# Layer 3's messages between the two steps of scaling: from SBUF into a PSUM bank

## The chip, the cores and the metric

The kernel runs on one core of a Trainium2 chip. The metric is the device time of one execution in microseconds (us), the median of several runs. TensorE (PE) does matmuls, VectorE (DVE), ScalarE (ACT) and GpSimd (POOL) do elementwise work; POOL also issues the gathers from tables in HBM (its indirect DMAs), and SyncE issues the plain DMAs.

## The reference, cut to what matters

Four graph layers follow one another over 6,250 nodes of 256 features and 100,000 edges that are sorted by their destination node. The change is in the last one, layer 3, an attention over edges with 4 heads of 64 features:

```python
h_fwd = h @ W_forward.T          # 6250 x 64
h_rev = h @ W_reverse.T
messages = h_fwd[src] * direction[:, 0:1] + h_rev[src] * direction[:, 1:2]
scores = jnp.einsum('ef,hf->eh', messages, attn_forward[0])
scores = jax.nn.leaky_relu(scores, negative_slope=0.2)
exp_scores = jnp.exp(scores - scores.max(axis=0, keepdims=True))
sum_exp = jax.ops.segment_sum(exp_scores, dst, num_segments=N)
norm = exp_scores / (sum_exp[dst] + 1e-10)
outs = [jax.ops.segment_sum(messages * norm[:, hd:hd + 1], dst, num_segments=N) for hd in range(H)]
```

Each edge has one message of 64 numbers; the four heads each scale it with their own weight, which makes 256 numbers, and these are summed per destination node.

## The kernel before, in words

Every layer first writes a table of node rows to HBM and then walks over the edges. The walk goes in 832 steps (`STEPS_PAD`), each of 128 edges, one to a partition, all with destinations in one tile of 128 nodes; 16 steps are a group (`GROUP`), so there are 52 groups. In layer 3 the stage of the edges is written by `mix_gpsimd`, `mix_scalar`, `mix_vector` and `mix_tensor`, one program for each engine, each in a fixed order, with semaphores between them.

One step `i` of layer 3 is this:

- POOL (line 1522) issues the gather of 128 table rows of 136 numbers (64 forward, 64 reverse, 4 and 4 scores) into `rows3`, which has room for three groups. It reads the row numbers from a column of `src_idx` in SBUF. From the fourth group on it waits for `mixed3` of 48 steps before, since it writes over that step's rows.
- ACT multiplies the reverse half by the edge's second attribute into `reverse` (`turn_about`, line 1575), copies the 4 weights beside the message's place in `scaled3` (line 1587) and makes the 128 x 128 matrix of destinations `hots3` (`hot`, lines 1564 and 1569).
- DVE makes the message (`mix`, line 1643): forward half times the first attribute plus `reverse`, 64 numbers per edge, into a ring of four, `message`.
- DVE scales the message by the heads' weights (the unlabelled `tensor_tensor` at line 1674): `message`, read four times over, times `weight3`, each weight read 64 times over, into `scaled3`: 256 numbers per edge.
- PE (line 1549) multiplies `hots3` by `scaled3` into PSUM bank `i % 6` (`BANKS` is 6, so banks 0 to 5), which sums the edges per node.
- DVE adds the bank to the sums of the node tile in SBUF (`add`, line 1662), two steps later (`LAG`).

The order on DVE within step `i` is: scale message `i` (line 1674), make message `i + 1` (line 1643), one piece of the next group's softmax chain (`chain`, lines 1606 to 1637), add step `i - 2` (line 1662). At the first step of a group the chain's first piece waits until the next group's 16 gathers have all landed (`landed3`), and `add` first rescales the running sums (lines 1654 and 1656). The chain also uses PSUM bank 7 (`top_bank`). Bank 6 is not used in this stage; it served the matmuls of the table before it.

After the last step, `close4_vector` and others divide, normalise and store the output.

Of the kernel before, what the change touches and what calls it, by code (L numbers as in the profile page):

```python
# [34 lines left out]
OUT3 = 64  # L35
# [179 lines left out]
def build(nc, io):  # L215
    ctx = ExitStack()
    with ctx:
# [15 lines left out]
        reg_b = scratch[:, 3 * GROUP * ROW3:3 * GROUP * ROW3 + 7488]  # L233
# [16 lines left out]
        psum = [ctx.enter_context(nc.psum_tensor(f"bank{k}", [P, 512], F32)) for k in range(8)]  # L250
# [1226 lines left out]
        WIDE3 = FEAT + HEADS3  # L1477
        rows3 = reg_a[:, 0:3 * GROUP * ROW3].rearrange("p (s f) -> p s f", f=ROW3)
        reverse = reg_b[:, 512:512 + 4 * OUT3].rearrange("p (s f) -> p s f", s=4)
        message = reg_b[:, 768:768 + 4 * OUT3].rearrange("p (s f) -> p s f", s=4)  # L1480
        weight3 = reg_b[:, 2048:2048 + 3 * GROUP * HEADS3].rearrange("p (g t h) -> p g t h", g=3, h=HEADS3)
        part_score = reg_b[:, 2304:2304 + 2 * GROUP * HEADS3].rearrange("p (k t h) -> p k t h", k=2, h=HEADS3)
        top, shrink3 = reg_b[:, 2500:2500 + HEADS3], reg_b[:, 2510:2510 + HEADS3]
# [3 lines left out]
        tops = reg_b[:, 2800:2800 + GROUPS * HEADS3].rearrange("p (g h) -> p g h", h=HEADS3)  # L1487
        hots3 = reg_b[:, 3100:3100 + 12 * P].rearrange("p (s f) -> p s f", s=12)
        scaled3 = reg_b[:, 4700:4700 + 4 * WIDE3].rearrange("p (s f) -> p s f", s=4)
        top_bank = psum[7]  # L1490

        m3_v = v_order.named("ones low")
# [392 lines left out]
```

## Time and profile before

| | us |
|---|---|
| median of 3 runs | 5997.77 |
| lowest and highest | 5993.94, 6015.3 |
| profiled execution, its own time | 6000.81 |
| its span | 5999.0 |
| layer 3's first gather starts, last gather starts (from the span's start) | 4770.6, 5879.3 |

| engine | busy us | share of the span |
|---|---|---|
| PE | 4283.5 | 71% |
| POOL | 4048.5 | 67% |
| DVE | 3532.0 | 59% |
| ACT | 2587.1 | 43% |

The shares are means over four layers with different limits; the stage that the change touches is the last fifth of the span. In rows of a timeline the first number is the start in us from the span's start and the second the duration in us.

### The profile page before, as it was taken

The page shows a single profiled execution, that of the slowest core. Times are in us where ns is not written, and L with a number is a line of the kernel's source. Part 1 is how long each engine was busy: PE and PEld are TensorE (multiplying, and loading weights), DVE is VectorE, ACT ScalarE, POOL GpSimd, SP SyncE. Part 2 cuts the span into 40 slices and gives each one's busy share as a digit, 9 for nine tenths or more (in the row PEclk, how much of TensorE's full clock was granted, in tenths as well). Part 3 has the DMA queues.
Part 4 walks back from the last instruction along what each step waited for, and adds up shares of the span by engine and source line. Part 5 has one row for each costly group of instructions (what it writes and reads, how often), then busy time and mean ns, then how long its engine had stood idle before and what let it go on. Part 6 is the DMA issues. An engine that isn't in the chain of part 4 may idle for free.

```text
span 5999.0 us, 80569 instructions
## 1 busy us (share of the span) xinstructions
PE 4283.5 (71%) x13320; PEld 2473.3 (41%) x13320; DVE 3532.0 (59%) x10770; ACT 2587.1 (43%) x7522; POOL 4048.5 (67%) x4116
## 2 busy tenths in 40 slices
PE   5798989855777777977777752777777756666662
PEld 3566766632333333643333321333333623333331
DVE  4677677883333334833333347666666667777777
ACT  1555565645444443444444452000000466666664
POOL 2777677736777775057777775777777377777772
PEclk8878787876767678977777765776777877777776
DMA  4333333323333332033333322333333122222221
GB/s 128 106 106 105 93 104 99 106 92 120 106 105 105 106 106 79 31 99 105 106 106 105 106 81 84 106 105 106 105 106 105 52 53 53 53 53 53 53 53 54
DMA packets 237711, 539.69 MB, mean 90 GB/s; under 512 B 68266, under 2 KB 120424, under 8 KB 237242
## 3 DMA queue, kind: packets, MB, share of 16 engines
q0 software_dynamic: 180176, 481.36, 29.1%
q1 hardware_dynamic: 57066, 53.19, 2.7%
q8 instruction: 159, 2.61, 0.2%
q14 instruction: 310, 2.54, 0.1%
HBM read 498.15 MB, written 36.14 MB: 89 GB/s over the span
## 4 chain that ended last, share of the span: by engine, by line
PE 41%; DMA 16%; issue 13%; DVE 12%; POOL 11%; ACT 5%; DVEq 1%; SPq 0%; ACTq 0%; POOLq 0%
PE bank L1153 18%; DMA scratch<-tab_x,src_idx 10%; PE bank L1549 10%; POOL scratch L1121 9%; PE bank L971 7%; DMA scratch<-tab_h,src_idx 5%; PE bank L828 4%; PE bank L816 2%; DVE reg_acc L1175 1%; DVE scratch L185 1%; DVE scratch L203 1%; DVE reg_acc L999 1%; POOL reg_x L724 1%; ACT scratch L1564 1%; DVE scratch L1265 1%
## 5 line engine op out<-in xcount | busy, mean ns | idle before, releaser
L1153 PE MATMUL bank<-scratch 128*128 x4980 | 2215.7, 567 | 953.1 <-SPq L1128 605.9
L1175 DVE TENSOR_TENSOR reg_acc<-reg_acc,bank 128x256 f32 x2490 | 1048.9, 421 | 1691.2 <-PE bank L1153 1659.9
L1153 PEld LDWEIGHTS bank<-scratch 128*128 128x128 f32 x4980 | 1093.8, 260 | 2074.4 <-issue 2004.7
L1121 POOL DMA_INDIRECT scratch<-tab_x,src_idx x1564 | 1483.5, 949 | 514.3 <-issue 277.4
L1134 ACT ACTIVATE scratch<-iota_row,dst_loc 128x128 f32<-128x128 f32 x1660 | 661.2, 400 | 1024.2 <-PE bank L1153 1004.1
L1121 POOL DMA_INDIRECT scratch<-tab_h,src_idx x782 | 741.1, 948 | 462.1 <-DMA tab_h<-reg_acc 224.0
L1522 POOL DMA_INDIRECT scratch<-tab_h,src_idx x832 | 856.3, 1029 | 263.8 <-issue 157.3
L724 POOL DMA_INDIRECT reg_x<-tab_h,src_idx x832 | 813.3, 978 | 297.6 <-issue 176.8
L1549 PE MATMUL bank<-scratch 128*128 128x260 f32 x1664 | 674.3, 522 | 429.2 <-issue 402.2
L971 PE MATMUL bank<-reg_x,scratch 128*128 128x265 f32 x1664 | 637.5, 492 | 100.7 <-DVE reg_x L1008 68.5
L1549 PEld LDWEIGHTS bank<-scratch 128*128 128x128 f32 x1664 | 325.3, 241 | 746.5 <-issue 708.2
L148 ACT COPY scratch<-bank 128x256 f32<-128x256 f32 (+1 forms) x196 | 76.9, 416 | 1005.5 <-PE bank L140 1005.5
L971 PEld LDWEIGHTS bank<-reg_x,scratch 128*128 128x128 f32 x1664 | 314.2, 226 | 246.3 <-DVE reg_x L1008 217.1
L999 DVE TENSOR_TENSOR reg_acc<-reg_acc,bank 128x265 f32 x832 | 353.8, 425 | 100.7 <-PE bank L971 88.0
L1008 DVE TENSOR_TENSOR reg_x<-reg_x 128x256 f32<-128x256 f32 x832 | 349.0, 420 | 0.4 <-ACT reg_x L781 0.4
L1662 DVE TENSOR_TENSOR reg_acc<-reg_acc,bank 128x260 f32 x832 | 340.4, 409 | 9.6 <-DVE reg_acc L1656 8.0
L1674 DVE TENSOR_TENSOR scratch<-scratch 128x256 f32<-128x256 f32 x832 | 341.9, 411 | 0.0
L1564 ACT ACTIVATE scratch<-iota_row,dst_loc 128x128 f32<-128x128 f32 x832 | 320.5, 386 | 0.0
L1159 DVE TENSOR_SCALAR scratch<-iota_row,dst_loc,edge_w 128x128 f32<-128x128 f32 x830 | 318.3, 384 | 0.0
L1587 ACT COPY scratch<-scratch 128x4 f32<-128x4 f32 x832 | 152.3, 183 | 325.8 <-PE bank L1549 320.7
L1575 ACT ACTIVATE scratch<-scratch,attr 128x64 f32<-128x64 f32 x832 | 285.9, 344 | 0.8 <-issue 0.7
L828 PEld LDWEIGHTS bank<-adst,scratch 128*128 128x128 f32 x1664 | 266.6, 239 | 39.4 <-issue 33.3
(230 smaller groups left out, 4423.8 us busy)
## 6 DMA issues: line engine op xcount, KB each, us to landing
scratch<-tab_h,src_idx POOLq DMA_INDIRECT x1614, 2.7
scratch<-tab_x,src_idx POOLq DMA_INDIRECT x1564, 2.7
reg_x<-tab_h,src_idx POOLq DMA_INDIRECT x832
reg_x<-in_x SPq DMA_DIRECT2D x12, 896.0 KB, 11.0
tab_h<-scratch SPq DMA_DIRECT2D x7, 924.0 KB, 4.5
tab_x<-reg_acc SPq DMA_DIRECT2D x7, 896.0 KB
tab_h<-reg_acc SPq DMA_DIRECT2D x7, 896.0 KB
tab_x<-reg_x SPq DMA_DIRECT2D x7, 896.0 KB
```

Of the source, the lines that this page charges most:

```text
L724: e.indirect_dma_start(rows0[:, t % (3 * S), 0:ROW0], None, tab_h0, bass.IndirectOffsetOnAxis(ap=src_idx[:, t:t + 1], axis=0)).then_inc(*g ...
L828: m = e.matmul(bank_d[:, t % S * H:(t % S + 1) * H], hots_t[:, c % 2, n * P:(n + 1) * P], adst[:, bass.DynSlice(tile_value(e, "tensor", t) ...
L971: e.matmul(psum[i % BANKS0][:, 0:W0_ROW], hots0[:, i % (2 * S), :], rows0[:, i % (3 * S), :], start=True, stop=True).then_inc(*product0.up)
L999: e.tensor_tensor(v, v, psum[i % BANKS0][:, 0:W0_ROW], ALU.add).then_inc(*added0.up)
L1008: e.tensor_tensor(v, v, bcast(row[:, FEAT:ROW0], 2, [P, H, D]), ALU.mult).then_inc(*weighted0.up)
L1121: e.indirect_dma_start(ring_rows[:, j % SLOTS, :], None, self.table, bass.IndirectOffsetOnAxis(ap=src_idx[:, j:j + 1], axis=0)).then_inc(* ...
L1134: e.activation(ring_hots[:, i % HOTS, :], iota_row[:, :], ACT.Abs, scale=-1.0, bias=dst_loc[:, i:i + 1]).then_inc(*self.far.up)
L1153: e.matmul(psum[i % EDGE_BANKS][:, 0:FEAT], ring_hots[:, i % HOTS, :], rows, start=True, stop=True).then_inc(*self.product.up)
L1175: e.tensor_tensor(v, v, psum[i % EDGE_BANKS][:, 0:FEAT], ALU.add).then_inc(*self.added.up)
L1522: e.indirect_dma_start(rows3[:, t % (3 * GROUP), :], None, tab_h3, bass.IndirectOffsetOnAxis(ap=src_idx[:, t:t + 1], axis=0)).then_inc(*go ...
L1549: e.matmul(psum[i % BANKS][:, 0:WIDE3], hots3[:, i % 12, :], scaled3[:, i % 4, :], start=True, stop=True).then_inc(*product3.up)
L1564: e.activation(hots3[:, i % 12, :], iota_row[:, :], ACT.Abs, scale=-1.0, bias=dst_loc[:, i:i + 1]).then_inc(*far3.up)
```

## The change

The ring `message` of four messages of 64 numbers moves from an SBUF region to PSUM bank 6, columns 0 to 255. Line 1643 then writes it to PSUM and line 1674 reads it from there; the weights, `scaled3` and `reverse` stay in SBUF. No instruction, wait or semaphore is added or taken away.

```diff
         reverse = reg_b[:, 512:512 + 4 * OUT3].rearrange("p (s f) -> p s f", s=4)
-        message = reg_b[:, 768:768 + 4 * OUT3].rearrange("p (s f) -> p s f", s=4)
         weight3 = reg_b[:, 2048:2048 + 3 * GROUP * HEADS3].rearrange("p (g t h) -> p g t h", g=3, h=HEADS3)
...
         scaled3 = reg_b[:, 4700:4700 + 4 * WIDE3].rearrange("p (s f) -> p s f", s=4)
+        message = psum[6][:, 0:4 * OUT3].rearrange("p (s f) -> p s f", s=4)
         top_bank = psum[7]
```

## Rows read from the trace of the kernel before

**Rows 1.** Busy time by window: layer 3's steady part, its last steps, the close.

```profile
core 0: us, PE busy (x) PEld busy (x) DVE busy (x) ACT busy (x) POOL busy (x), PEclk, DMA share, GB/s
4815.00:5880.00 1065.00, 661.55 (x1746) 333.03 (x1746) 798.14 (x3037) 671.58 (x2697) 822.34 (x797) 0.77 0.23 53
5880.00:5915.00 35.00, 24.42 (x65) 12.13 (x65) 30.49 (x110) 19.28 (x79) 0.26 (x1) 0.80 0.01 2
5915.00:5999.00 84.00, 0.00 (x0) 0.00 (x0) 62.97 (x176) 27.94 (x58) 17.54 (x4) 0.50 0.23 76
```

**Rows 2.** Groups of instructions on POOL, window 4815 to 5880.

```profile
L1522 POOL DMA_INDIRECT scratch<-tab_h,src_idx x797 | 823.1, 1033 | 243.0 <-issue 146.9 <-DVE scratch L1643 96.0
```

**Rows 3.** The waits, same window.

```profile
DVE scratch L1606 <- DMA scratch<-tab_h,src_idx: 236.9, 49, 5.5
POOL scratch L1522 <- issue: 146.9, 482, 0.3
POOL scratch L1522 <- DVE scratch L1643: 96.0, 315, 0.3
```

**Rows 4.** Groups on POOL, window 4771 to 4801, before DVE mixes.

```profile
L1522 POOL DMA_INDIRECT scratch<-tab_h,src_idx x25 | 23.6, 946 | 17.8 <-DMA tab_h<-scratch 10.5 <-issue 7.3
```

**Rows 5.** Timeline of POOL in one group of steps.

```profile
5199.28 0.99 POOL L1522 DMA_INDIRECT scratch<-tab_h,src_idx  x1 [0.30 <-issue]
...
5205.69 1.25 POOL L1522 DMA_INDIRECT scratch<-tab_h,src_idx  x1 [0.30 <-issue]
...
5208.49 1.30 POOL L1522 DMA_INDIRECT scratch<-tab_h,src_idx  x1 [0.30 <-DVE scratch L1643]
5210.10 0.95 POOL L1522 DMA_INDIRECT scratch<-tab_h,src_idx  x1 [0.30 <-DVE scratch L1643]
5211.35 1.31 POOL L1522 DMA_INDIRECT scratch<-tab_h,src_idx  x1 [0.31 <-issue]
5212.97 0.95 POOL L1522 DMA_INDIRECT scratch<-tab_h,src_idx  x1 [0.30 <-DVE scratch L1643]
...
5220.61 0.95 POOL L1522 DMA_INDIRECT scratch<-tab_h,src_idx  x1 [0.30 <-issue]
```

**Rows 6.** Timeline of DVE, what ran as those gathers began.

```profile
5199.23 0.21 DVE L1612 TENSOR_TENSOR scratch<-scratch 128x64 f32<-128x64 f32 x1
...
5205.70 0.41 DVE L1674 TENSOR_TENSOR scratch<-scratch 128x256 f32<-128x256 f32 x1
...
5208.56 0.41 DVE L1674 TENSOR_TENSOR scratch<-scratch 128x256 f32<-128x256 f32 x1
...
5210.03 0.40 DVE L1662 TENSOR_TENSOR reg_acc<-reg_acc,bank 128x260 f32 x1
...
5211.44 0.41 DVE L1674 TENSOR_TENSOR scratch<-scratch 128x256 f32<-128x256 f32 x1
...
5212.84 0.41 DVE L1662 TENSOR_TENSOR reg_acc<-reg_acc,bank 128x260 f32 x1
...
5220.47 0.28 DVE L1643 SCALAR_TENSOR_TENSOR scratch<-scratch,attr 128x64 f32<-128x64 f32 x1
```

**Rows 7.** The page's costliest groups: the other gathers and the layer-0 scaling.

```profile
L1121 POOL DMA_INDIRECT scratch<-tab_x,src_idx x1564 | 1483.5, 949 | 514.3 <-issue 277.4
...
L724 POOL DMA_INDIRECT reg_x<-tab_h,src_idx x832 | 813.3, 978 | 297.6 <-issue 176.8
...
L1008 DVE TENSOR_TENSOR reg_x<-reg_x 128x256 f32<-128x256 f32 x832 | 349.0, 420 | 0.4 <-ACT reg_x L781 0.4
```

**Rows 8.** Groups on DVE, window 4815 to 5880.

```profile
L1674 DVE TENSOR_TENSOR scratch<-scratch 128x256 f32<-128x256 f32 x798 | 327.9, 411 | 0.0
L1662 DVE TENSOR_TENSOR reg_acc<-reg_acc,bank 128x260 f32 x797 | 325.9, 409 | 8.2 <-DVE reg_acc L1656 7.7 <-PE bank L1549 0.2
L1643 DVE SCALAR_TENSOR_TENSOR scratch<-scratch,attr 128x64 f32<-128x64 f32 x798 | 215.1, 270 | 0.0
```

**Rows 9.** Tile view of the banks on DVE (ns: least, median, most; first and last start).

```profile
L1455 DVE TENSOR_TENSOR scratch<-bank,reg_w x49: 389/392/424, 4676.7 to 4761.5; 128x256 f32<-128x256 f32 x49
```

## The prediction

> **What bounds the kernel now.** I read the stages first, since the change touches one of four layers. Layer 3's walk over the edges runs from the first gather at 4770.6 us to about 5915 us. In its steady part of 1065 us [rows 1] POOL is the busiest engine with 822 us, DVE has 798, ACT 672, PE 662. The reader should not stop at 77% busy: the groups of POOL [rows 2] show 797 gathers of 1033 ns, with 243 us of idle before them, which is 0.305 us each. 797 x (1.033 + 0.305) = 1066 us, the whole window. The longest such idle is 0.3 us, whether the row blames "issue" or line 1643 [rows 3], so it is a constant gap between two gathers and no wait for data: POOL goes from one gather to the next without a stop, and the stage lasts as long as 832 of them.
>
> The waits say the same from the other side. DVE's one large wait is at line 1606, the first piece of the chain, for the gathers of the next group: 236.9 us in 49 times, 4.8 us for each group [rows 3]. A group takes 16 x 1.338 = 21.4 us, so DVE has 16.6 us of work in it and then waits for rows. The page's chain of waits names PE for much of this stage; there PE is idle 38% of the window [rows 1], so I go by the queue that never stops, POOL's.
>
> The next question is why a gather takes 1033 ns here. Before DVE begins to mix, the same line takes 946 ns [rows 4]; in layers 1 and 2, 949 ns [rows 7]. The single rows differ in kind: most are 0.94 or 0.95 us, some 1.2 to 1.3. I laid POOL's rows [rows 5] beside DVE's [rows 6]:
>
> - The gather at 5205.69 took 1.25; the scaling of line 1674 started at 5205.70 and ended at 6.11. The gather ended at 6.94, 0.83 after it.
> - 5208.49 took 1.30; line 1674 ran 8.56 to 8.97; the gather ended 0.82 after it.
> - 5211.35 took 1.31; line 1674 ran 11.44 to 11.85; the gather ended 0.81 after it.
> - 5210.10 and 5212.97 took 0.95, with line 1662 running from 10.03 and from 12.84: as long an instruction (0.40 us), writing SBUF too, but with one of its two inputs in PSUM.
>
> So a stretched gather is held until line 1674 is done with its reading, and goes on for 0.8 us from there; an undisturbed one needs 0.95 in all, so what is held is something 0.1 us after its start. What tells line 1674 from line 1662 is two tensor inputs in SBUF against one, and the gather itself reads its row numbers from SBUF. The Trainium skill, "SBUF — State Buffer", section "Who interferes with whom", says that a VectorE instruction with two SBUF inputs contends with a GpSimd instruction that reads SBUF, and that one with at most one SBUF input, outside the two-port modes, does not. By that rule the trace agrees: 1.25 to 1.31 against 0.95.
>
> **The change part by part.** *Line 1674 with one input in PSUM, on POOL.* The cost that it can remove is the mean stretch: 1033 - 946 = 87 ns for each of 797 gathers, 69 us [rows 2, 4]. With the other passes' 949 ns as the floor [rows 7] it would be 67 us. Not all of it is line 1674's. The gather at 5199.28 took 0.99 with line 1612 starting at 5199.23, 64 numbers from two SBUF inputs: 0.04 us, at most once in a group, 50 x 0.04 = 2 us, and this stays. Line 1643 keeps its two SBUF inputs as well (rows and `reverse`). At 5220.61 a gather began while line 1643 ran from 5220.47 to 0.75 and took 0.95 all the same, so a short instruction leaves little; I keep another 2 us for it. The saving is then 69 - 2 - 2 = 65 us. Nothing else has to move: POOL's next gather needs the message of 48 steps before, three groups back, and no gather waits for it now (0.3 us at most [rows 3]).
>
> *Does POOL remain the bound?* A group would take 16 x (0.950 + 0.305) = 20.1 us. DVE's 16.6 us still fit, with 3.5 us over, 0.22 us for each step. ACT's 672 us and PE's 662 us in 797 steps [rows 1] are 0.84 and 0.83 us for each step, under 1.25.
>
> *Line 1674 on DVE.* The nearest rows with an input in PSUM are line 1662 with 260 numbers, 409 ns [rows 8], and line 1455 with 256, 392 ns [rows 9], against line 1674's 411 ns. The change is between -0.02 and nothing; I take nothing. It would be hidden by the wait at line 1606 but for the 32 or so steps after the last gather, where DVE works without waiting for rows (30.5 us busy of 35 [rows 1]): 32 x 0.02 = 0.6 us.
> The Trainium skill, "VectorE: DVE Perf Modes", section on the TRN2 errata, has a fixed 120 cycles for a PSUM source against 58 for SBUF, a rule that speaks against the change: 62 cycles at 0.96 GHz are 0.065 us, by my estimate 54 us of DVE time over 832 steps, of which only the last 32 steps, 2 us, would lie bare. The trace does not agree: 409 ns with a PSUM input, 411 without.
>
> *Line 1643 writes to PSUM.* No row shows DVE writing to a bank. From below, nothing gained (270 ns stays, as it has its own inputs); from above I take that it costs as much as the widest of the two SBUF-only kinds here, line 1674's 411 ns: +0.14 us a step. That is under the 0.22 us of slack, so it shows only in the last 32 steps, 4.5 us. I take nothing, since reads of banks cost no more than reads of SBUF here. Line 1674 needs the message of line 1643 that started a chain piece and an add before it (0.5 us), which covers a late landing of that write.
>
> *Bank 6.* PE writes banks 0 to 5 and 7 in this stage and no one else touches 6, so nothing new waits for a bank.
>
> *Sum.* 6000.8 - 65 = 5936 us for an execution like the profiled one. That one lies 3 us above the median of the runs, so the median should be 5998 - 65 = 5933; with up to a microsecond or so of DVE cost in the bare end, 5934.
>
> **The rivals.**
>
> *Line 1643 takes the hold over.* It still reads two SBUF tensors 832 times and its phase against POOL may now fall badly. If its 270 ns held a gather as line 1674's 411 ns do, both the chance of a hit and the length of the hold would shrink by 270/411, so (0.66)^2 = 0.43 of the stretch would be there: 30 of 69 us. Gain 65 - 28 = 37, time 5961. Layer 0 gives it some support: there gathers take 978 ns [rows 7] beside a two-input scaling of 420 ns. Against it: the row at 5220.61. A group has 16 such instructions and only 16 gathers, as with line 1674. Chance 0.12.
>
> *The hold is not in the read.* If it were in line 1674's write to SBUF or in how POOL is served while `weight3` is read with repeats, moving the message changes nothing: 5998, within half a per cent. For it: only correlation in rows. Against: line 1662 writes as many numbers to SBUF and holds nothing. The Trainium skill's page "SBUF — State Buffer", same section, also reports a probe in which `tensor_tensor` did not stall a DMA issued from GpSimd, and infers that making descriptors needs the write interface; if that held here the time would stay. The rows at 5205.69, 5208.49 and 5211.35 speak against it. Chance 0.06.
>
> *Slower: DVE becomes the bound.* If the path from line 1643's write to line 1674's read through PSUM were long, each step would wait for `mixed3`, and with it line 1643, the chain and the add queued behind, then PE. It decides from 0.22 us per step. To be slower than now by over 30 us a group must last 21.4 + 0.6 = 22.0 us, so DVE would need (22.0 - 16.6)/16 = 0.34 us more a step, twice my upper bound for line 1643. At 0.38 us a group is 22.7 us, and the time 5998 + 52 x 1.3 = 6066. Chance 0.03.
>
> **How the numbers follow.** Forecast 0.79, line 1643 takes over 0.12, no effect 0.06, slower 0.03. The forecast's own range: 69 us saved and runs 5 us lower than their median give 5924; 4.5 us for line 1643 in the end and twice the remaining stretch (4 us) give 5942. The range of eight in ten takes in the first rival: 5924 to 5962. Half a per cent of this kernel is 30 us, about what a measurement can tell from no change. Forecast and first rival are both faster by more than that, so faster 0.91, same 0.06, slower 0.03.
>
> **What the profile after would show.** Line 1522's mean falls from 1033 to about 950 ns, its gap stays 0.305; the last gather starts near 5813 us instead of 5879. Rows over 1.1 us are gone; the few stretched ones are at 1.0 and lie on lines 1612 or 1643. Line 1674 stays within 20 ns of 411. DVE's wait at line 1606 shrinks from 4.8 to about 3.5 us a group. I am wrong if gathers of 1.1 us and over remain beside line 1643 (first rival), if the mean stays 1033 (second), or if line 1606's wait vanishes and DVE shows idle time before line 1674 (third).

## The result and the profile after

The changed kernel took 5952.24 us in the median of 14 runs, against 5995.85 us for 14 runs of the kernel before on the same chips: a ratio of 0.9919, with a 95% interval from 0.9897 to 0.9942. That is 44 us faster, and the interval spans 35 to 62 us. Forecast were 5934 us and a gain of 64, in a range from 5924 to 5962. The time lies inside that range, but above 5942, the upper end that the prediction gave for its own mechanism; only the first rival's 5961 carried the range so far.

The profiled execution took 5964.45 us, its span is 5962.7 us. The groups of the page that answer to [rows 7] and to the table of before, gathers and the two scalings:

```profile
L1121 POOL DMA_INDIRECT scratch<-tab_x,src_idx x1564 | 1480.0, 946 | 514.0 <-issue 286.4
...
L724 POOL DMA_INDIRECT reg_x<-tab_h,src_idx x832 | 810.0, 974 | 324.1 <-issue 180.7
L1522 POOL DMA_INDIRECT scratch<-tab_h,src_idx x832 | 799.0, 960 | 263.7 <-issue 184.1
```

Layer 3's gather fell from 1029 ns over all 832 to 960 ns; the other gathers of the kernel are within 4 ns of what they took before. The idle time before line 1522 is 263.7 us, as before (263.8): POOL still goes from gather to gather with its gap of about 0.3 us and nothing else. So the stage's walk, from the start of its first gather to that of its last, should be shorter by 832 x 0.069 = 57 us. The source view of the line (least, median and most ns, first and last start) has it:

```profile
L1522 POOL DMA_INDIRECT scratch<-tab_h,src_idx x832: 940/944/1244, 4791.8 to 5843.0; - x167
```

5843.0 - 4791.8 = 1051.2 us, against 1108.7 before: 57.5 us less. The same view for line 1674, first the kernel before, then the one after, shows that the stage's other end followed:

```profile
L1674 DVE TENSOR_TENSOR scratch<-scratch x832: 404/406/467, 4801.6 to 5912.3; 128x256 f32<-128x256 f32 x167
```

```profile
L1674 DVE TENSOR_TENSOR scratch<-bank,scratch x832: 404/405/424, 4822.7 to 5875.9; 128x256 f32<-128x256 f32 x167
```

The last scaling starts 33.0 us after the last gather before and 32.9 us after it now. From first gather to last scaling the stage went from 1141.7 to 1084.1 us.

Groups of DVE in the steady part of the stage after, window 4815 to 5840, to be laid beside [rows 8] and, for the last one, [rows 3]:

```profile
L1674 DVE TENSOR_TENSOR scratch<-bank,scratch 128x256 f32<-128x256 f32 x799 | 326.6, 409 | 0.0
L1662 DVE TENSOR_TENSOR reg_acc<-reg_acc,bank 128x260 f32 x797 | 326.3, 409 | 8.8 <-DVE reg_acc L1656 7.8 <-PE bank L1549 0.9
L1643 DVE SCALAR_TENSOR_TENSOR bank<-scratch,attr 128x64 f32<-128x64 f32 x800 | 220.2, 275 | 5.7 <-ACT scratch L1575 5.7
...
L1606 DVE TENSOR_TENSOR scratch<-scratch,attr 128x64 f32<-128x64 f32 x50 | 11.6, 233 | 197.6 <-DMA scratch<-tab_h,src_idx 197.6
```

Line 1674 costs 409 ns with its message in PSUM, 411 before; line 1643 costs 275 ns writing to PSUM, 270 before. DVE still waits for rows at line 1606, 4.0 us a group.

**Why this profile's span is only 36 us shorter.** Layer 3's first gather starts at 4791.8 us, 21 us later than before, ahead of any changed instruction. The time was lost in layer 0, whose windows read, before and then after:

```profile
131.00:1240.00 1109.00, 954.60 (x4500) 722.06 (x4500) 803.65 (x2689) 624.79 (x1771) 813.35 (x832) 0.81 0.38 103
```

```profile
131.00:1240.00 1109.00, 968.22 (x4424) 738.27 (x4424) 789.91 (x2641) 614.37 (x1744) 793.65 (x816) 0.78 0.37 101
```

The mean granted TensorE clock was 0.81 and then 0.78, and after the same 1109 us POOL had issued 816 gathers of layer 0 instead of 832. In layer 0 POOL waited 137.6 us for PE (line 971), 114.9 before, and those 23 us are about what is missing. In the profiles of the experiments below that were taken on chips of this pace, all with the same code up to layer 3, the first gather of line 1522 starts anywhere from 4753.2 to 4784.9 us. Five of those seven kernels contain the change, and their layer 3 begins at 4753.2 to 4784.9 us, so the change does not by itself put that start at 4791.8. I read the 21 us as such a spread. In this pair of profiles the span is shorter by 57.6 us in the stage and longer by 21.2 ahead of it; from the last scaling to the end both take 86.7 to 86.8 us.

### The profile page after: what moved, and what is told of

It reads as the page before. It is cut to its first block, busy times and chain, and to the rows that moved or that the text cites. A ratio compares the mean times of both kernels' runs of the same rounds, so it can differ in the third digit from the quotient of the medians.

```text
span 5962.7 us, 80569 instructions
## 1 busy us (share of the span) xinstructions
PE 4323.6 (73%) x13320; PEld 2508.8 (42%) x13320; DVE 3526.4 (59%) x10770; ACT 2585.1 (43%) x7522; POOL 3982.4 (67%) x4116
## 4 chain that ended last, share of the span: by engine, by line
PE 43%; DMA 15%; DVE 12%; issue 12%; POOL 11%; ACT 5%; DVEq 1%; SPq 0%; ACTq 0%; POOLq 0%
PE bank L1153 18%; DMA scratch<-tab_x,src_idx 10%; PE bank L1549 10%; POOL scratch L1121 9%; PE bank L971 8%; DMA scratch<-tab_h,src_idx 5%; PE bank L828 4%; PE bank L816 2%; DVE reg_acc L1175 1%; DVE scratch L185 1%; DVE scratch L203 1%; DVE reg_acc L999 1%; ACT scratch L1564 1%; POOL reg_x L724 1%; ACT scratch L1569 1%
## 5 line engine op out<-in xcount | busy, mean ns | idle before, releaser
L1121 POOL DMA_INDIRECT scratch<-tab_h,src_idx x782 | 739.3, 945 | 462.3 <-DMA tab_h<-reg_acc 224.4
L1522 POOL DMA_INDIRECT scratch<-tab_h,src_idx x832 | 799.0, 960 | 263.7 <-issue 184.1
L971 PE MATMUL bank<-reg_x,scratch 128*128 128x265 f32 x1664 | 659.4, 509 | 96.7 <-DVE reg_x L1008 56.4
L971 PEld LDWEIGHTS bank<-reg_x,scratch 128*128 128x128 f32 x1664 | 328.2, 234 | 242.1 <-DVE reg_x L1008 209.2
L1674 DVE TENSOR_TENSOR scratch<-bank,scratch 128x256 f32<-128x256 f32 x832 | 340.2, 409 | 0.0
L828 PEld LDWEIGHTS bank<-adst,scratch 128*128 128x128 f32 x1664 | 283.0, 252 | 39.2 <-issue 32.3
L828 PE MATMUL bank<-adst,scratch 128*128 x1664 | 271.1, 291 | 20.1 <-issue 18.3
```

The lines of the kernel that those rows point to most:

```text
L828: m = e.matmul(bank_d[:, t % S * H:(t % S + 1) * H], hots_t[:, c % 2, n * P:(n + 1) * P], adst[:, bass.DynSlice(tile_value(e, "tensor", t) ...
L971: e.matmul(psum[i % BANKS0][:, 0:W0_ROW], hots0[:, i % (2 * S), :], rows0[:, i % (3 * S), :], start=True, stop=True).then_inc(*product0.up)
L1121: e.indirect_dma_start(ring_rows[:, j % SLOTS, :], None, self.table, bass.IndirectOffsetOnAxis(ap=src_idx[:, j:j + 1], axis=0)).then_inc(* ...
L1522: e.indirect_dma_start(rows3[:, t % (3 * GROUP), :], None, tab_h3, bass.IndirectOffsetOnAxis(ap=src_idx[:, t:t + 1], axis=0)).then_inc(*go ...
```

## The experiments

All compare layer 3's gathers: their mean, their walk, and which are stretched. "Walk" is first gather start to last gather start.

**1. Which input, and read or write.** Two kernels start from the one before. In the first the messages stay in SBUF and the weights go to PSUM:

```diff
+        weight_bank = psum[6][:, 0:2 * GROUP * HEADS3].rearrange("p (g t h) -> p g t h", g=2, h=HEADS3)
...
+                if k == 0:
+                    e.tensor_copy(weight_bank[:, g % 2], weight3[:, g % 3]).then_inc(*banked3.up)
+                    e.wait_ge(*banked3(g))
                 e.tensor_tensor(scaled3[:, s, 0:FEAT].rearrange("p (h d) -> p h d", h=HEADS3),
                                 bcast(message[:, s, :], 1, [P, HEADS3, OUT3]),
-                                bcast(weight3[:, g % 3, k, :], 2, [P, HEADS3, OUT3]),
+                                bcast(weight_bank[:, g % 2, k, :], 2, [P, HEADS3, OUT3]),
                                 ALU.mult).then_inc(*weighted3.up)
```

> The kernel before, its messages in SBUF, but VectorE copies each group's weights once into PSUM bank 6, and line 1674 reads its weights from there. Theory (the count of SBUF inputs of line 1674 decides, not which one): the gathers' mean is 955 to 965 ns as in the changed kernel, the walk about 1051 us against 1109, the time 40 to 60 us under the kernel before. Rival (it matters that the message moved, for its place or for its reading straight after it was written): gathers stay at 1029 ns, the walk at 1109 us, the time unchanged.

In the second only the output of line 1674 goes to PSUM. PE then multiplies a `scaled3` that is set to zero once, so this kernel's sums leave the messages out:

```diff
+        out_bank = psum[6][:, 0:512].rearrange("p (s h d) -> p s h d", s=2, h=HEADS3)
...
+                if i >= 2:
+                    e.wait_ge(*weighted3(i - 2))
-                e.tensor_tensor(scaled3[:, s, 0:FEAT].rearrange("p (h d) -> p h d", h=HEADS3),
+                e.tensor_tensor(out_bank[:, i % 2],
                                 bcast(message[:, s, :], 1, [P, HEADS3, OUT3]),
                                 bcast(weight3[:, g % 3, k, :], 2, [P, HEADS3, OUT3]),
                                 ALU.mult).then_inc(*weighted3.up)
```

> The kernel before, with both inputs of line 1674 in SBUF as there, but its 256 numbers are written to PSUM bank 6 instead of scaled3. PE multiplies by a scaled3 that is zero, so the sums leave the messages out. Theory (the hold is in the read of two SBUF inputs): the gathers' mean stays at 1020 to 1040 ns, the walk near 1109 us. Rival (the hold is in the write to SBUF): the mean falls to 945 to 960 ns and the walk to 1045 to 1055 us.

The gathers in the pages' groups, weights in PSUM and then the output in PSUM:

```profile
L1524 POOL DMA_INDIRECT scratch<-tab_h,src_idx x832 | 801.7, 964 | 263.7 <-issue 185.3
```

```profile
L1523 POOL DMA_INDIRECT scratch<-tab_h,src_idx x832 | 853.5, 1026 | 263.8 <-issue 151.5
```

With the weights in PSUM the gathers take 964 ns, the walk is 1054.0 us, and the time is 5956.18 us (10 runs, ratio 0.9929, from 0.9903 to 0.9955): the whole of the gain, with the messages where they were. With the output in PSUM and both inputs in SBUF nothing is gained: 1026 ns, a walk of 1105.8 us, and a time of 6001.88 us (one run) beside 5991.94 for the kernel before. So the hold comes from reading two SBUF inputs; where the result goes, and which of the inputs leaves SBUF, does not matter. Nor do the repeats in the weights: in the changed kernel line 1674 still reads `weight3` from SBUF, each weight 64 times over, and holds nothing. That the part of the gather which is held is its own read of the row numbers is an inference; no run here takes that read away.

**2. What is left.** After the change the gathers' mean is 960 ns, and the least disturbed take 940 to 944. The reverse half goes to PSUM too, so that line 1643 has one SBUF input:

```diff
-        reverse = reg_b[:, 512:512 + 4 * OUT3].rearrange("p (s f) -> p s f", s=4)
+        reverse = [psum[4][:, 0:OUT3], psum[5][:, 0:OUT3]]
+        BANKS3 = 4
...
-                if i >= 4:
-                    e.wait_ge(*mixed3(i - 4))
-                e.mul(reverse[:, i % 4, :], rows3[:, i % (3 * GROUP), OUT3:2 * OUT3],
+                if i >= 2:
+                    e.wait_ge(*mixed3(i - 2))
+                e.mul(reverse[i % 2], rows3[:, i % (3 * GROUP), OUT3:2 * OUT3],
...
-                                       in1=reverse[:, i % 4, :], op0=ALU.mult, op1=ALU.add).then_inc(*mixed3.up)
+                                       in1=reverse[i % 2], op0=ALU.mult, op1=ALU.add).then_inc(*mixed3.up)
```

> The changed kernel with the reverse half in PSUM as well: ACT writes it in turns into banks 4 and 5 (a ring of two, and the products' ring cut from six banks to four), so that line 1643 too has one SBUF input. Theory (any VectorE instruction with two SBUF inputs holds the gather's read of its row numbers; what is left in the changed kernel is line 1643): the gathers' mean falls from 960 to about 943 ns, all gathers above 1.1 us are gone, and the walk from first to last gather is 12 to 14 us shorter than the changed kernel's 1051 us; about 70 us shorter than before. Rival (what is left comes from the chain's small instructions, or the gathers have a spread of their own): the mean stays near 960 ns and the walk at 1051 us. Second rival (the shorter rings of reverse and of the products become a wait): the wait at line 1606 vanishes and the walk is longer than 1051 us.

```profile
L1523 POOL DMA_INDIRECT scratch<-tab_h,src_idx x832: 940/945/1073, 4784.9 to 5825.1; - x167
```

The walk is 1040.2 us, 11.0 us shorter than after the change (12 to 14 had been expected), no gather takes more than 1.073 us, and the mean is 947 ns. The time was 5922.06 us in 6 runs (ratio to the kernel before 0.9874, from 0.9835 to 0.9913), the fastest version of the study; by its time alone it can't be told from the changed kernel, since the intervals overlap, and the 11 us rest on the walk. What is left is 2.5 us in all when the stretches above the median are added up, and most of it lies beside the chain's own small instructions.

**3. Two in a row.** In the timeline after, 33 gathers of 1.15 us or more are left between 4830 and 5845 us (189 before, between 4815 and 5880), 1.22 to 1.24 us each. POOL and DVE around one of them:

```profile
4926.07 1.24 POOL L1522 DMA_INDIRECT scratch<-tab_h,src_idx  x1 [0.30 <-issue]
```

```profile
4926.07 0.27 DVE L1643 SCALAR_TENSOR_TENSOR bank<-scratch,attr 128x64 f32<-128x64 f32 x1
4926.26 0.20 DVE L1636 TENSOR_TENSOR scratch<-scratch 128x64 f32<-128x64 f32 x1
4926.40 0.14 DVE L1637 TENSOR_TENSOR scratch<-scratch 128x4 f32<-128x4 f32 x1
```

(Line 1637, on 4 numbers, has two SBUF inputs as well; the gather ends 0.77 us after it.) And around one without line 1636:

```profile
5092.24 1.03 POOL L1522 DMA_INDIRECT scratch<-tab_h,src_idx  x1 [0.30 <-issue]
```

```profile
5092.18 0.28 DVE L1643 SCALAR_TENSOR_TENSOR bank<-scratch,attr 128x64 f32<-128x64 f32 x1
```

The second gather ends at 5093.27, 0.81 us after line 1643, the distance that was read for line 1674 in [rows 5, 6]. The first ends at 4927.31, which is 0.97 us after line 1643 but 0.85 after line 1636, so it was let in only behind line 1636. All depends on a hundredth of a microsecond: of the 44 gathers that begin within 0.06 us of line 1643 where line 1636 follows, the 11 that begin 0.014 us or more ahead of it take 0.94 us, and the 33 that begin later take 1.22 to 1.24. The next experiment puts lines 1636 and 1637 ahead of line 1643:

```diff
-                if i + 1 < STEPS_PAD:
-                    mix(i + 1)
                 if g + 1 < GROUPS:
                     chain(g + 1, k)
+                if i + 1 < STEPS_PAD:
+                    mix(i + 1)
```

> The changed kernel with VectorE's piece of the chain ahead of line 1643 instead of behind it, so that line 1643 is followed by line 1662, which has one input in PSUM. In the changed kernel 33 gathers of about 1.24 us all began with line 1643 and had line 1636, with two SBUF inputs again, right behind it. Theory (a gather that is held by one such instruction loses the read to the next one when that follows at once): the gathers of over 1.15 us go away, the stretches left are under 0.12 us, the mean is about 950 ns, the walk 6 to 10 us shorter than 1051 us. Rival (line 1643 alone holds for up to 0.3 us): some 30 or more gathers of over 1.15 us remain and the mean stays at 960 ns.

```profile
L1522 POOL DMA_INDIRECT scratch<-tab_h,src_idx x832 | 799.5, 961 | 263.7 <-issue 188.9
```

The gathers of 1.24 us did go: 2 are over 1.15 us instead of 33. But the mean is 961 ns and the walk 1051.8 us, where 950 ns and 6 to 10 us less had been expected. The swap does not separate the instructions, it only turns their order round, and 27 gathers of 1.11 to 1.13 us have come in place of the 33. One of them, POOL first, then DVE:

```profile
4908.62 1.13 POOL L1522 DMA_INDIRECT scratch<-tab_h,src_idx  x1 [0.30 <-issue]
```

```profile
4908.64 0.20 DVE L1636 TENSOR_TENSOR scratch<-scratch 128x64 f32<-128x64 f32 x1
4908.77 0.14 DVE L1637 TENSOR_TENSOR scratch<-scratch 128x4 f32<-128x4 f32 x1
4908.84 0.27 DVE L1643 SCALAR_TENSOR_TENSOR bank<-scratch,attr 128x64 f32<-128x64 f32 x1
```

It ends at 4909.75, 0.84 us after line 1637 and 0.64 after line 1643: it was let in ahead of line 1643. The kernel before shows the same. There line 1643 stands right behind line 1674, after the one of [rows 6] at 5205.70 like this:

```profile
5206.04 0.27 DVE L1643 SCALAR_TENSOR_TENSOR scratch<-scratch,attr 128x64 f32<-128x64 f32 x1
```

The gather of [rows 5] ended at 5206.94, 0.83 us after line 1674 and 0.63 after line 1643. So a second instruction with two SBUF inputs prolongs the hold in one order and not in the other, and why is not shown. Besides, 164 gathers in the window show 0.96 us or more in their rows instead of 111. That the sum of the stretches came out the same (14 us above the median in both) may be chance; one swap does not show that the order never matters. The time was 5927.01 us in 4 runs (ratio 0.9892, from 0.9842 to 0.9941); its walk being that of the changed kernel, I put nothing of that to the swap, and its layer 3 began at 4753.2 us.

**4. One more instruction on DVE.** Three kernels add an instruction behind line 1643 of the changed kernel, its output unused; `fill_a` and `fill_b` are 64 SBUF numbers each, set to one. The first, with one input in PSUM:

```diff
+        fill_a, fill_b = reg_b[:, 768:832], reg_b[:, 832:896]
...
                 if i + 1 < STEPS_PAD:
                     mix(i + 1)
+                if i >= 2:
+                    e.wait_ge(*padded3(i - 2))
+                e.tensor_tensor(pad_out[:, i % 2, 0:OUT3], message[:, s, :], fill_b, ALU.add).then_inc(*padded3.up)
```

The second reads `fill_a` in SBUF instead of `message`. The third is the first with 256 numbers. They ran first on a chip where all was slow:

> The changed kernel with one more VectorE add of 64 numbers behind line 1643 in every step, one input in PSUM (the message) and one in SBUF, its output not used. It costs VectorE about 0.13 to 0.2 us a step, under the 0.22 us that it has to spare in each. Theory: the gathers' mean stays at 945 to 965 ns and the walk at 1045 to 1055 us, with the wait at line 1606 down from 4 to about 1 us a group; with a one-PSUM instruction behind line 1643 few or no gathers exceed 1.15 us. Rival (VectorE has no such slack, it is close to being the bound): the walk grows by 100 us or more.

> As pad_psum, but both inputs of the added 64-number add lie in SBUF. VectorE's time is the same. Theory (two SBUF inputs hold the gather's read): there are twice as many short holders, and they come in pairs, so more gathers are over 1.1 us than with pad_psum; the mean is 970 to 1000 ns and the walk 10 to 35 us longer than with pad_psum. Rival (short instructions do not hold): the mean is that of pad_psum within 3 ns.

> As pad_psum with 256 numbers, again one input in PSUM: about 0.34 us more of VectorE in a step, over the 0.22 us to spare. Theory: VectorE becomes the bound, the wait at line 1606 nearly vanishes, POOL waits for messages, a group takes about 16.6 + 16 x 0.34 = 22.0 us and the walk about 1140 us, longer than before the change although each gather stays at 945 to 965 ns. Rival (gathers set the pace whatever VectorE has to do): the walk stays at 1051 us.

The times there were 7000.52, 7018.2 and 7017.94 us, beside 7003.5 for the kernel before, one run each. The walks were 1225.7, 1225.0 and 1223.9 us, with POOL idle for over 436 us before its gathers instead of 264: something else sets the pace on that chip (experiment 5). For the walk these runs say nothing. For the hold they do, 948 ns against 962. On a chip of the usual pace:

> The kernel of pad_psum once more, since the kernel before took 7003 us on the chip of that run, and in all three padded kernels gathers were then held up on POOL for something else than here. On a chip where the kernel before takes about 6000 us, theory: the gathers' mean 945 to 965 ns, the walk 1038 to 1055 us, the wait at line 1606's piece of the chain down to about 1 to 2 us a group. Rival (VectorE has no slack): the walk grows by 50 us or more.

> The kernel of pad_sbuf once more, for the same reason. There its gathers took 962 ns against 948 with pad_psum, which is half of what I had expected. Theory: on this chip again 12 to 30 ns more in the mean than pad_psum2, with gathers over 1.15 us that pad_psum2 has not, and the walk longer than pad_psum2's by 832 times that, 10 to 25 us. Rival: the same mean within 3 ns.

> The kernel of pad_wide once more, for the same reason. Theory: VectorE becomes the bound, POOL waits for messages, and the walk is about 1140 us (1100 to 1160), longer than the 1109 us of the kernel before, although each gather takes only 945 to 955 ns. Rival (gathers set the pace whatever VectorE has to do): the walk stays at 1040 to 1055 us.

The source view of the gathers, one input in PSUM, both in SBUF, and the wide one:

```profile
L1525 POOL DMA_INDIRECT scratch<-tab_h,src_idx x832: 940/944/1083, 4779.1 to 5820.1; - x167
```

```profile
L1525 POOL DMA_INDIRECT scratch<-tab_h,src_idx x832: 940/944/1346, 4784.6 to 5837.2; - x167
```

```profile
L1525 POOL DMA_INDIRECT scratch<-tab_h,src_idx x832: 938/944/1181, 4773.5 to 5855.4; - x167
```

- One input in PSUM: walk 1041.0 us, mean 948 ns, no gather over 1.083 us. With 0.14 us a step more on DVE the stage is not longer than after the change but 10 us shorter, and DVE's wait for a group's rows is down from 4.0 to 1.6 us: DVE's slack of 0.22 us a step was real. The 10 us are mostly luck of phase. Only 4 gathers begin within 0.06 us of line 1647 (here the mix) in a step with line 1640 (the chain's 64 numbers, two SBUF inputs), instead of 44. These 4 take 1.05 to 1.06 us and end 0.82 to 0.83 us after line 1647, so they were let in at the new instruction; held to the end of line 1640, 0.48 us after their start, they would have taken 1.3.
- Both in SBUF: walk 1052.6 us, mean 962 ns, the longest gather 1346 ns. The same time on DVE and the same place, 11.6 us longer: this is the price of one more short instruction with two SBUF inputs, 14 ns for each gather. The theory's 12 to 30 ns holds at its lower end; the first expectation, a mean of 970 to 1000 ns, did not, with 962 on both chips.
- 256 numbers: the walk of the gathers is 1081.9 us, not the 1140 expected, and no longer the measure: POOL runs up to three groups ahead of DVE. The last scaling tells the stage's length,

```profile
L1678 DVE TENSOR_TENSOR scratch<-bank,scratch x832: 403/405/431, 4815.5 to 5873.6; 128x256 f32<-128x256 f32 x167
```

```profile
L1678 DVE TENSOR_TENSOR scratch<-bank,scratch x832: 403/404/432, 4804.5 to 5917.8; 128x256 f32<-128x256 f32 x167
```

with both inputs in SBUF and then with 256 numbers. The wide one has 5917.8 - 4773.5 = 1144.3 us from first gather to last scaling, against 1141.7 in the kernel before and 1084.1 after. That is 52 groups of 16.6 + 16 x 0.34 = 22.0 us, and DVE is busy 995 of 1005 us between 4815 and 5820. The time was 6006.69 us, beside 5970.96 for the kernel before (one run each). Here the waits of POOL name what the third rival had feared:

```profile
POOL scratch L1525 <- DVE bank L1647: 172.1, 442, 1.5
```

**5. Another chip.** The last two kernels were meant to set the changed kernel beside that of experiment 2 on one chip.

> The changed kernel as it is, on one chip with all_psum_again. Theory: its ratio to the kernel before is that of the first measurement, 0.992 (0.989 to 0.995), and the gathers' mean 958 to 963 ns. Rival (the 57 us from layer 3 are partly given back in the earlier layers by the change itself, which is why the profiled execution gained only 36): the first gather of layer 3 starts again some 20 us later than in the profile of the kernel before, at 4790 us.

> The kernel of all_psum again, for a comparison with the changed kernel on one chip. Theory: 11 us faster than changed_again, that is a ratio of 0.990 where that has 0.992, with the gathers' mean at 947 ns and a walk of 1040 us. Rival: no difference in time that the runs can tell.

They came to the slow chip. The kernel before took 7018.03 us there (23 runs), the changed kernel 7011.33 (11 runs, ratio 0.9986, from 0.9977 to 0.9995), the other 7008.16 (12 runs, 0.9986, from 0.9976 to 0.9997). The changed kernel's gathers:

```profile
L1522 POOL DMA_INDIRECT scratch<-tab_h,src_idx x832: 938/944/1289, 5648.8 to 6877.7; - x167
its engine sat idle before it (us, times) until:
  issue: 241.4, 671
  DVE bank L1643: 143.4, 129
  remote: 53.2, 31
...
who waited for it (us, times):
  DVE scratch L1606: 29.8, 2
```

They are as short as on the other chips (952 ns in the mean), but the walk is 1228.9 us, since POOL sat idle 448.5 us before them. DVE waits for rows only twice there, 29.8 us in all, against 52 times and 222.9 us in the profile after: on that chip POOL is not what bounds the stage. An excerpt of the timeline (all engines) shows pauses of PE, ACT and DVE at one time, and POOL's following 2 us later:

```profile
6302.36 0.16 DVE L1637 TENSOR_TENSOR scratch<-scratch 128x4 f32<-128x4 f32 x1
...
6303.35 0.26 ACT L1558 ACTIVATE scratch<-scratch 128x64 f32<-128x64 f32 x1 [1.62 <-DVE scratch L1637]
...
6304.18 0.43 DVE L1662 TENSOR_TENSOR reg_acc<-reg_acc,bank 128x260 f32 x1 [1.67 <-issue]
...
6305.04 0.68 PE L1549 MATMUL bank<-scratch 128*128 128x260 f32 x2 [1.63 <-issue]
...
6306.41 0.94 POOL L1522 DMA_INDIRECT scratch<-tab_h,src_idx  x1 [1.58 <-DVE bank L1643]
```

There a quicker gather is worth next to nothing, 7 us by the medians. Both ratios miss what was expected (0.992 and 0.990). What makes that chip pause stays open, and whether the 21 us that the profiled execution lost in layer 0 are chance could not be tested there either.

## Why the prediction was right

- **POOL bounds the stage, 832 gathers with a gap of 0.305 us.** Right. Walk and mean moved together: 69 ns x 832 = 57 us, walk 57.5 us. And where DVE was made dearer by 0.14 us a step the stage did not grow.
- **Line 1674 holds the gather by its two SBUF inputs.** Right, shown from three sides (experiment 1 and the change itself). No stretch in the profile after lies on line 1674. This agrees with the Trainium skill, "SBUF — State Buffer", section "Who interferes with whom", for two SBUF inputs against an instruction of GpSimd that reads SBUF. It does not agree with the probe that the section reports, in which `tensor_tensor` did not stall a DMA, nor with what it infers from it: here the gather took 1029 ns with both inputs of line 1674 in SBUF and 960 with one.
- **The remnant.** This is the term of the sum that was mis-sized: "I keep another 2 us for it". With line 1643's input in PSUM the walk was 11 us shorter, so line 1643, alone and together with line 1636 behind it, held 11 us. I had judged by one gather, at 5220.61. It ended at 5221.56, 0.81 us after line 1643: the usual distance, at which a gather of 0.94 us that begins late enough loses nothing. The same arithmetic goes far to explain why two in a row cost more than twice one: the first 0.13 us (0.94 - 0.81) of a hold are free, and only once. With 2 + 11 us for the remnant the sum would have been 69 - 13 = 56 us, against 57.5 measured in the stage.
- **The sign of being wrong.** The prediction wrote that rows over 1.1 us would be gone, and that it was wrong if such gathers remained beside line 1643. There are 33, all beside that line, and the mean is 960 ns instead of 950. So the first rival was right in kind and too large in size: it gave line 1643 30 us, and the runs 11.
- **DVE and the message's way through PSUM.** Right: 409 against 411 ns, 275 against 270, the bare end 32.9 against 33.0 us. The third rival's threshold held as well, met by an instruction put there for it: a group of 22.0 us, and slower than before.
- **The time.** The stage gained 57.5 us, nearer the forecast's 65 than the first rival's 37; the median gained 44, and its 5952 us are nearer the rival's 5961 than the forecast's 5934. That the time lies within the stated range is therefore in part luck. The 57.5 us are inside the interval of 35 to 62, and I don't explain the difference to 44; layer 3's first gather alone starts up to 39 us apart from one profile to the next (4753.2 to 4791.8).

## What to carry to other kernels

Where gathers issued by GpSimd follow one another without a stop, look at their single durations, not at the mean, and lay the long ones beside VectorE's rows: each VectorE instruction with two SBUF inputs is a candidate, and one input moved to a free PSUM bank (here either did) took the hold away at no cost to VectorE that showed. Count the short ones too. Layer 0's gathers still take 974 ns in the mean, beside line 1008 with two SBUF inputs; whether the same move pays there was not tried. Before working on a mean over many instructions, ask what it is a mixture of: here 1033 ns was about 945 for most and 1.15 to 1.5 us for nearly a quarter.

## What the runs showed of the hardware that was not expected

- The kernel before took 5971 to 5996 us on some chips and 7018 us on another (1.17 times 5996). In the changed kernel there the gathers' median is the same 944 ns and that of line 1674 is 418 against 405, and there are pauses, of 1.2 to 1.7 us in the rows shown. The change was worth 0.8% on the former and 0.1% on the latter.
- One short VectorE instruction (64 numbers, two SBUF inputs) stretched a gather to 1.03 us, line 1643 with line 1636 behind it to 1.24 us, and three of 64 numbers in a row to 1.33 us, though in the other order line 1643 adds nothing (experiment 3). The last is from the kernel with both inputs of the added instruction in SBUF, first POOL, then DVE; the gather ends 0.84 us after line 1640.

```profile
4920.64 1.33 POOL L1525 DMA_INDIRECT scratch<-tab_h,src_idx  x1 [0.30 <-issue]
```

```profile
4920.60 0.27 DVE L1647 SCALAR_TENSOR_TENSOR bank<-scratch,attr 128x64 f32<-128x64 f32 x1
4920.79 0.20 DVE L1686 TENSOR_TENSOR scratch<-scratch 128x64 f32<-128x64 f32 x1
4920.93 0.20 DVE L1640 TENSOR_TENSOR scratch<-scratch 128x64 f32<-128x64 f32 x1
4921.06 0.14 DVE L1641 TENSOR_TENSOR scratch<-scratch 128x4 f32<-128x4 f32 x1
```

With the added instruction's input in PSUM, in the same step of a group, the gather is let in between and ends 0.82 us after line 1647:

```profile
4874.11 1.05 POOL L1525 DMA_INDIRECT scratch<-tab_h,src_idx  x1 [0.30 <-issue]
```

```profile
4874.07 0.27 DVE L1647 SCALAR_TENSOR_TENSOR bank<-scratch,attr 128x64 f32<-128x64 f32 x1
4874.27 0.20 DVE L1686 TENSOR_TENSOR scratch<-bank,scratch 128x64 f32<-128x64 f32 x1
4874.40 0.20 DVE L1640 TENSOR_TENSOR scratch<-scratch 128x64 f32<-128x64 f32 x1
```
